# Layer norm statistics of four of sixteen token tiles moved from VectorE to ScalarE, in the routing rounds of a Golay and top-2 expert kernel

## The chip, the cores and the metric

The kernel runs on one core of one Trainium2 chip. The metric is the device time of one execution in microseconds (us). Three executions of the kernel before took 1242.68, 1247.49 and 1249.14 us; their median is 1247.49 us. The engines are TensorE (PE), VectorE (DVE), ScalarE (ACT), GpSimd (POOL) and SyncE (SP, which here only starts transfers).

## The reference

`x` has 16 x 1024 tokens of 512 features. Every token is normed, goes through a frequency filter with a 24-bit code correction, and through its two best of eight experts:

```
xn = (x - mean(x)) / sqrt(var(x) + 1e-5)
x1 = real(ifft(fft(xn) * filt))                     # filt from the first 1024 values of xn
bits = sigmoid(x1 @ W_el + b_el) > 0.5              # 24 bits, Golay-corrected
s = x1 + corrected @ W_le + b_le
probs = softmax(xn @ router_w.T)                    # 8 experts, top 2 kept
g = silu(sum over the 2 of (xn @ expert_e + prob_e) * weight_e)
out = x + s * g
```

## The kernel before, in words

The 16384 tokens are 128 tiles of 128 tokens. There are three stages.

**Set-up**, up to some 30 us: filter tables, weights of the router.

**Routing rounds**, up to some 305 us. There are R = 8 rounds of U = 4 steps, a step being a block of GT = 4 tiles (128 x 2048 values, 1 MB). Every engine runs its own `step1(i, k)` for round i and step k, in program order, and waits on semaphores only.

- SP loads block k of round i into `xbuf[:, k]` (`load`, L378). There are only four block buffers, so a load waits until TensorE has turned the block that lies there (`t1_done`) and until its statistics are taken (`stats_ready`). In rounds 2 to 7 the order is block 0, block 1, one expert's weights, block 2, block 3.
- TensorE, in `step1(i, k)`: turns the first two tiles of the next block (L1266), does the product with the router and latent weights of this block (`logits`, L1306), turns the other two tiles of the next block, and turns the result back (L1315). `logits` waits until ScalarE has copied all four turned tiles of its block. At k = 2 it also ranks the tokens of the round before (`rank`, L1323), for which it waits for `pairs` from VectorE.
- ScalarE copies the turned tiles of the next block from PSUM (`turn_copy`, L586), two before and two after the copy of this block's result (`latT_copy`, L632). Between steps it has the norms of the expert weights (`norm`, L592; one in step 0 of each of rounds 1 to 5), the exponentials (L636) and the root of the variance (L670).
- VectorE takes the statistics of a tile by one `bn_stats` (`stat`, L907). In step 0 it runs `choose(i - 1)` (L971 to L999, bits and top 2 of the round before), a chain of small operations, and puts the twelve `stat` of blocks 1 to 3 of round i between them. In step 1 it works out the variances (`deviations`) and then combines one expert's weights (`halves`). In step 2 `place(i - 1)` gives each token its slot (L1038), with the four `stat` of block 0 of the next round beside it; it waits for `rank`. Step 3 is `weigh(i - 1)`.
- GpSimd writes the token numbers into a table in DRAM by sixteen small scatters a round (L493), as soon as the slots of the round are there.

Behind the last round GpSimd's last scatters, two gathers of that table and some index work lead to the first gather of the next stage.

**Expert tiles**, from some 305 us to the end: 28 extra and 128 main tiles of tokens gathered by expert pair. The change doesn't touch them. They use `inf2` as a buffer, which the routing rounds don't use.

Of the kernel before, what the change touches and what calls it, by code (L numbers as in the profile page):

```python
# [10 lines left out]
BF16 = mybir.dt.bfloat16  # L11
# [13 lines left out]
GT = 4  # L25
U = 4
# [52 lines left out]
def build(nc, x_in, W_el, b_el, W_le, b_le, router_w, experts, consts, out):  # L79
# [37 lines left out]
    with ctx:  # L117
# [3 lines left out]
        def sem(name):  # L121
# [116 lines left out]
        to_tile = latT[:, 1, 0:2 * NT].rearrange("p (h t) -> p h t", h=2)  # L238
        onehot = xT4[:, :, :, :].rearrange("p b c n -> p (b c n)")[:, 0:T * 2 * NE].rearrange(
            "p (t s e) -> p t s e", s=2, e=NE)  # L240
        info_bits = info[:, :, 16:64].bitcast(BF16).rearrange("p t (g c) -> p t g c", g=3)


# [32 lines left out]
        def sems(names):  # L276
            return [sem(x) for x in names.split()]
# [13 lines left out]

        t1_done, t1_copied, mm1_done, latT_copied, back_done, lat_copied = sems(
            "t1_done t1_copied mm1_done latT_copied back_done lat_copied")
        stats_ready, aggr_ready, var_ready, sd_ready, newton, rstd_ready = sems(
            "stats_ready aggr_ready var_ready sd_ready newton rstd_ready")
        route_a, route_c, route_d, dx_ready, exp_ready, corr_ready, bits_copied = sems(
# [30 lines left out]
        def after(eng, s, v):  # L327

            if isinstance(v, int) and v <= 0:
                return  # L330
            eng.wait_ge(s, v)
# [41 lines left out]
        @block.sync  # L373
        def _(sp):
            def load(i, k):
                after(sp, t1_done, GT * ((i - 1) * U + k + 1))
                after(sp, stats_ready, (i - 1) * U + k + 1)
                sp.dma_start(xbuf[:, k], x_tiles[:, i, k * GT:(k + 1) * GT, :]).then_inc(ld_x[k], 16)  # L378

            def load_expert(e):  # L380
                if e == LH:
                    sp.wait_ge(pool_halves, 1)
                after(sp, wpm_ready, e - LH)
                after(sp, norm_ready, e - LH + 1)
                sp.dma_start(raw[:, e % LH], experts[e].rearrange("(c p) o -> p c o", p=P)).then_inc(ld_w[e % LH], 16)

            sp.dma_start(x01, x_rows[0:2, :].rearrange("n e -> (n e)").partition_broadcast(P)).then_inc(ld_x01, 16)
            sp.dma_start(rtr, router_w).then_inc(ld_router, 16)
            load(0, 0)
            sp.dma_start(cst[:, :], consts).then_inc(ld_cst, 16)  # L390
            sp.dma_start(welraw, W_el.rearrange("(c p) n -> p c n", p=P)).then_inc(ld_small, 16)
            sp.dma_start(bel[:, :], b_el.partition_broadcast(P)).then_inc(ld_small, 16)
            load(0, 1)
            sp.wait_ge(zeroed, 1)
            for g in range(3):
                sp.dma_start(wle[32 * g:32 * g + GOLAY_N, :], W_le).then_inc(ld_small, 16)
                sp.dma_start(wle[32 * g + GOLAY_N:32 * g + GOLAY_N + 1, :], b_le.rearrange("(a e) -> a e", a=1)).then_inc(ld_small, 16)
            load_expert(0)
            load_expert(1)
            load(0, 2)  # L400
            load(0, 3)
            sp.wait_ge(ld_cst, 16)
            table = pair_tokens.rearrange("(p h r) c -> p h (r c)", p=P, h=FILLS)
            for h in range(FILLS):
                sp.dma_start(table[:, h], cst[:, 0:TROWS // FILLS].bitcast(I32)).then_inc(far_stored, 16)
            load(1, 0)
            load(1, 1)
            load(1, 2)
            load_expert(2)
            load(1, 3)  # L410
            load_expert(3)
            for i in range(2, R):
                for k in range(U):
                    load(i, k)
                    if k == 1 and i + 2 < NE:
                        load_expert(i + 2)

            def turn_main(i, k):
                m, b = (i - XR) * U + k, k % 2
                sp.wait_ge(split_ready, i * U + k + 1)  # L420
                sp.sem_inc(split_seen, 1)
                sp.wait_ge(bits_in, m + 1)
                sp.sem_inc(bits_seen, 1)
                if first_main(i) and k < 2:
                    sp.wait_ge(x_done, NX - 4 + k + 1)
                else:
                    sp.wait_ge(y_done, m - 1)
                sp.sem_inc(y_seen, 1)
                sp.dma_start_transpose(facing[b], parts[b]).then_inc(turned[b], 16)

            def extra_sum(i, k):
                m = (i - XR) * U + k
                if not first_main(i):
                    sp.wait_ge(t_ready, m - U + 1)
                    sp.sem_inc(sum_seen, 1)
                which = sp.value_load(tile_exp[0:1, 2, bass.ds(m, 1)], min_val=0, max_val=NX - 1)
                sp.dma_start(ebuf[:, k], extra_dram[bass.ds(which, 1)].rearrange("o p e -> p (o e)")).then_inc(ld_e[k], 16)

            def step(i, k, last=False):
                if not (last and k + 2 >= U):  # L440
                    turn_main(*at(i, k, 2))
                    extra_sum(*at(i, k, 2))
            for n in range(NX):
                if NX <= n + 3 < NX + 2:
                    turn_main(*at(n // U, n % U, 3))
                sp.wait_ge(acc_ready, n + 1)
                sp.dma_start(extra_dram[n], acc2[:, n % 2]).then_inc(extra_stored[n % 2], 16)
            sp.wait_ge(tiles_ready, 3)
            for b in range(2):
                sp.wait_ge(extra_stored[b], 16 * (NX // 2))  # L450
            extra_sum(XR, 0)
            extra_sum(XR, 1)
            main_rounds(sp, step)
# [126 lines left out]
        def _(act):  # L580
# [69 lines left out]

            NORM_AT = {(0, 2): 2, (1, 0): 3, (2, 0): 4, (3, 0): 5, (4, 0): 6, (5, 0): 7}

            def step1(i, k, last):
                ahead = not (last and k + 1 >= U)
                if ahead and not turned_early(i, k):
                    turn_copy(*at(i, k, 1), 0)
                    turn_copy(*at(i, k, 1), 1)
                latT_copy(i, k)
                if ahead and not turned_early(i, k):
                    turn_copy(*at(i, k, 1), 2)  # L660
                    turn_copy(*at(i, k, 1), 3)
                if i >= 2 and k == 0:
                    info_store(i - 2)
                if (i, k) in NORM_AT:
                    norm(NORM_AT[i, k])
                if i >= 1 and k == 1:
                    exps(i - 1)
                if k == 2:
                    act.wait_ge(var_ready, i + 1)
                    nc.scalar.activation(rt1[:, 1], rt1[:, 0], ACT.Sqrt).then_inc(sd_ready, 1)  # L670
                    if i >= 1:
                        bits_copy(i - 1)
# [82 lines left out]
        def _(dve):  # L755
# [103 lines left out]
                            ALU.subtract).then_inc(c_lo_ready, 1)  # L859

            V.tensor_copy(nbefore[:, :], nbefore_c)
            V.tensor_copy(used[:, :], region_c).then_inc(sort_init, 1)
            dve.wait_ge(iota_ready, 1)
            link(V.tensor_copy(tokf[:, :], tok[:, 1, :]))
# [46 lines left out]
            def deviations(i):  # L911


                dve.wait_ge(stats_ready, U * (i + 1))
                mean_e, sq_e, mean_o, sq_o = (st6[:, :, c] for c in (1, 2, 4, 5))
                V.tensor_tensor(dev[:, 0], mean_e, mean_o, ALU.subtract)
                V.tensor_tensor(dev[:, 1], sq_e, sq_o, ALU.add)
                V.tensor_tensor(dev[:, 2], mean_e, mean_o, ALU.add).then_inc(aggr_ready, 1)
                dve.wait_ge(aggr_ready, 2 * i + 1)
                V.scalar_tensor_tensor(dev[:, 3], dev[:, 0], 0.25, dev[:, 0], ALU.mult, ALU.mult)  # L920
                V.tensor_scalar(dev[:, 1], dev[:, 1], 1.0 / E, EPS, ALU.mult, ALU.add).then_inc(aggr_ready, 1)
                dve.wait_ge(aggr_ready, 2 * i + 2)
                V.tensor_tensor(rt1[:, 0], dev[:, 1], dev[:, 3], ALU.add).then_inc(var_ready, 1)
# [125 lines left out]
            def step1(i, k, last):  # L1049
                following = NONE if last else tiles_of(i + 1, 0)  # L1050
                if i >= 1 and k == 0:
                    choose(i - 1, beside=tiles_of(i, 1) + tiles_of(i, 2) + tiles_of(i, 3))
                if k == 1:
                    if i == 0:
                        for tile in tiles_of(i, 1) + tiles_of(i, 2) + tiles_of(i, 3):
                            tile()
                    deviations(i)
                    if i + 2 < NE:
                        halves(i + 2 if i else 1)
                if i >= 1 and k == 2:  # L1060
                    place(i - 1, (i - 1) % 2, (i - 1) // 2, beside=following)
                if k == 3:
# [386 lines left out]
```

## Time and profile before

| | |
|---|---|
| median of three runs | 1247.49 us |
| profiled execution, its own time | 1248.74 us |
| its span on the core | 1246.9 us |
| busy in the span: TensorE, VectorE, GpSimd, ScalarE | 90%, 87%, 70%, 41% |
| granted TensorE clock, mean | 0.954 |

The span is the time between the first and the last recorded instruction; 1.8 us of the execution's time lie outside of it. Shares over the whole span say little here, since the change sits in the routing rounds alone, which are the stretch from about 30 to 243 us. So the profile is read by stretches and by the order in time of single rows.

### The profile page before, as it was taken

To read this page: it belongs to the slowest core of one execution; us is meant where nothing else is said; L and a number is where in the kernel's file an instruction comes from. 1 tells how busy PE (TensorE), PEld (TensorE's weight loads), DVE (VectorE), ACT (ScalarE), POOL (GpSimd) and SP (SyncE) were. 2 spreads that over 40 slices of the span, in tenths; PEclk is the share of its full clock that TensorE was granted. 3 is DMA by queue.
4 is the path that set the end of the run, shared out by engine and by line. 5 is a ranking of instruction groups with operands and counts; after the bars stand their busy time and mean duration, and the time that the engine had idled before them with its cause. 6 is when DMAs were issued, how large, how long until landed. Compare 5 with 4: busy or idle time off the path is not lost. (4 is left out here: it accounts for less than half of the span.)

```text
span 1246.9 us, 26774 instructions
## 1 busy us (share of the span) xinstructions
PE 1122.4 (90%) x6265; PEld 608.3 (49%) x6266; DVE 1089.1 (87%) x2625; ACT 509.0 (41%) x1151; POOL 877.0 (70%) x873
## 2 busy tenths in 40 slices
PE   5998889700799999999999999999999999999996
PEld 4554555400355455555555554555555555555553
DVE  6799979992888689989999998999999899999985
ACT  4576556560577333323333333333333333333332
POOL 1126654765888378778888887888888788888874
PEclk8999889955799999999999999999999999999999
DMA  8659999300465576666666666666666666666664
GB/s 320 238 192 200 195 168 214 64 18 24 129 185 184 143 167 174 173 168 177 172 171 176 176 173 170 169 172 177 174 174 172 167 178 172 178 170 173 177 168 108
DMA packets 217433, 208.75 MB, mean 167 GB/s; under 512 B 166783, under 2 KB 166783, under 8 KB 213298
## 3 DMA queue, kind: packets, MB, share of 16 engines
q1 hardware_dynamic: 184370, 124.31, 42.2%
q0 software_dynamic: 31872, 79.79, 21.6%
q10 hardware_dynamic: 1152, 4.19, 1.4%
q8 instruction: 17, 0.28, 0.1%
q14 instruction: 22, 0.18, 0.1%
HBM read 123.36 MB, written 47.12 MB: 137 GB/s over the span
## 5 line engine op out<-in xcount | busy, mean ns | idle before, releaser
L1366 PE MATMUL banks<-w_hi,arena 128*128 (+1 forms) x1136 | 431.6, 380 | 9.5 <-DMA arena<-arena 5.0
L1367 PE MATMUL banks<-w_lo,arena 128*128 (+1 forms) x1136 | 431.3, 380 | 0.0
L1368 PE MATMUL banks<-w_hi,arena 128*128 (+1 forms) x1136 | 431.1, 379 | 0.0
L700 ACT ACTIVATE arena<-xbuf,inf 128x512 f16<-128x512 f32 x156 | 112.6, 722 | 509.6 <-DVE xbuf L1168 509.6
L516 POOL DMA_INDIRECT inf<-token_info,gidx x156 | 194.7, 1248 | 54.1 <-issue 54.1
L514 POOL DMA_INDIRECT xbuf<-in_L_attn_x,gidx x156 | 176.3, 1130 | 77.4 <-issue 67.0
L493 POOL DMA_INDIRECT pair_tokens<-tok,slot x128 | 133.8, 1045 | 122.7 <-DVE slot L1038 81.0
L554 POOL TENSOR_TENSOR xbuf<-xbuf 128x512 f32<-128x512 f32 x128 | 162.7, 1271 | 40.1 <-DVE xbuf L1237 35.9
L1366 PEld LDWEIGHTS banks<-w_hi,arena 128*128 128x128 f16 x1136 | 111.2, 98 | 136.7 <-issue 15.0
L1368 PEld LDWEIGHTS banks<-w_hi,arena 128*128 128x128 f16 x1136 | 111.4, 98 | 131.5 <-issue 0.8
L520 POOL DMA_INDIRECT out<-xbuf,sidx x128 | 140.4, 1097 | 40.7 <-issue 40.4
L1367 PEld LDWEIGHTS banks<-w_lo,arena 128*128 128x128 f16 x1136 | 111.2, 98 | 117.1 <-issue 0.6
L1164 DVE TENSOR_TENSOR xbuf<-xbuf 128x256 f32<-128x256 f32 x156 | 141.6, 908 | 13.7 <-DMA inf<-token_info,gidx 13.7
L1174 DVE SCALAR_TENSOR_TENSOR arena<-xbuf,inf,arena 128x512 f16<-128x512 f32 x156 | 117.0, 750 | 19.2 <-ACT arena L700 13.0
L1306 PE MATMUL banks<-xT,wcat 128*128 128x512 f32 x256 | 120.8, 616 | 0.8 <-issue 0.4
L1217 DVE SCALAR_TENSOR_TENSOR arena<-banks,cab,arena 128x512 f32<-128x512 f32 x128 | 95.6, 747 | 13.1 <-PE banks L1368 12.3
L1237 DVE TENSOR_TENSOR xbuf<-xbuf,arena 128x512 f32<-128x512 f32 x128 | 88.7, 693 | 20.7 <-DVE xbuf L1231 7.7
L1208 DVE SCALAR_TENSOR_TENSOR arena<-banks,cab,arena 128x512 f32<-128x512 f32 x128 | 95.9, 749 | 7.9 <-DMA arena<-extra_sums 4.1
L1231 DVE TENSOR_TENSOR xbuf<-xbuf 128x256 f32<-128x256 f32 x256 | 97.5, 422 | 4.4
L734 ACT ACTIVATE arena<-arena,inf 128x512 f32<-128x512 f32 x128 | 91.1, 712 | 3.8 <-DVE arena L1217 3.8
L907 DVE BATCH_NORM_STATS2 st<-xbuf 128x6 f32<-128x512 f32 x128 | 86.0, 684 | 7.1 <-DMA xbuf<-in_L_attn_x 7.1
L1266 PE MATMUL banks<-ident,xbuf 128*128 128x128 f32 x512 | 74.1, 293 | 17.0 <-DMA xbuf<-in_L_attn_x 16.8
(284 smaller groups left out, 1713.5 us busy)
## 6 DMA issues: line engine op xcount, KB each, us to landing
xbuf<-in_L_attn_x SPq DMA_DIRECT2D x32, 1024.0 KB, 13.7
arena<-extra_sums SPq DMA_DIRECT2D x128, 256.0 KB, 2.7
arena<-in_L_ffn_expert_weights SPq DMA_DIRECT2D x8, 1024.0 KB, 11.7
extra_sums<-arena SPq DMA_DIRECT2D x28, 256.0 KB, 2.1
token_info<-info ACTq DMA_DIRECT2D x8, 512.0 KB, 12.8
xbuf<-in_L_attn_x,gidx POOLq DMA_INDIRECT x156, 3.6
inf<-token_info,gidx POOLq DMA_INDIRECT x156, 2.8
pair_tokens<-tok,slot POOLq DMA_INDIRECT x128
```

The source lines that it names most:

```text
L493: pool.indirect_dma_start(out=pair_slots, out_offset=bass.IndirectOffsetOnAxis(ap=slot[:, buf, t:t + 1], axis=0), in_=tok[:, buf, t:t + 1] ...
L514: pool.indirect_dma_start(out=x2[:, k], out_offset=None, in_=x_rows, in_offset=tokens, bounds_check=N - 1, oob_is_err=False).then_inc(ld_x ...
L516: pool.indirect_dma_start(out=inf2[:, k], out_offset=None, in_=info_dram, in_offset=tokens, bounds_check=N - 1, oob_is_err=False).then_inc ...
L520: pool.indirect_dma_start(out=out_rows, out_offset=bass.IndirectOffsetOnAxis(ap=sidx[:, k:k + 1], axis=0), in_=o2[:, k % 2], in_offset=Non ...
L554: G.tensor_tensor(o2[:, b], sg2[:, b], x2[:, k], ALU.add).then_inc(o_ready, 1)
L700: nc.scalar.activation(hi4[ring(i, k)], uv2[:, b], ACT.Copy, scale=inf2[:, k, 1:2]).then_inc(hi_ready, 1)
L1164: V.tensor_tensor(raw2[:, b, 0:H], x2[:, k, 0:H], x2[:, k, H:E], ALU.add).then_inc(raw_ready, 1)
L1174: V.scalar_tensor_tensor(lo4[ring(i, k)], uv2[:, b], inf2[:, k, 1:2], hi4[ring(i, k)], ALU.mult, ALU.subtract).then_inc(split_ready, 1)
L1306: last = mm(psum[:, 2], wcat[:, c], xT4[:, k % 2, c], start=(c == 0), stop=(c == C - 1))
L1366: mm(ps, hi[:, c], wh, start=(c == 0), stop=False)
L1367: mm(ps, hi[:, c], wl, start=False, stop=False)
L1368: end = mm(ps, lo[:, c], wh, start=False, stop=(c == C - 1))
```

## The change

Of the sixteen tiles of a round, the four of block 3 get their mean and their sum of squared deviations from ScalarE. For each, one pass `Copy` with scale 1/512 adds up to the mean, and a second pass `Square` of (mean - x) adds up to the squared deviations. The values that the passes write go to `inf2`, which nothing reads then. `bn_stats` gives two means and two sums for a tile (even and odd values); ScalarE's passes give one of each, so the mean is written twice and the second sum stays zero.

The passes for tiles 0 and 1 of the block stand in ScalarE's step 0, those for tiles 2 and 3 in its step 1, around the copies that were there. VectorE's step 1 does `halves` first and `deviations` after it, the latter with waits for ScalarE's passes.

```
         def _(sp):
             def load(i, k):
                 after(sp, t1_done, GT * ((i - 1) * U + k + 1))
-                after(sp, stats_ready, (i - 1) * U + k + 1)
+                if k < U - 1:
+                    after(sp, stats_ready, (i - 1) * (U - 1) + k + 1)
+                else:
+                    after(sp, squares_ready, GT * i)
...
+            def tile_mean(i, q):
+
+                if q == 0:
+                    act.wait_ge(ld_x[U - 1], 16 * (i + 1))
+                    after(act, var_ready, i)
+                after(act, squares_ready, GT * i + q)
+                nc.scalar.activation(squares, xbuf[:, U - 1, q], ACT.Copy, scale=1.0 / E,
+                                     accum_out=st6[:, SHARE + q, 1:2]).then_inc(means_ready, 1)
+
+            def tile_square(i, q):
+
+                act.wait_ge(means_ready, GT * i + q + 1)
+                nc.scalar.activation(squares, xbuf[:, U - 1, q], ACT.Square, bias=st6[:, SHARE + q, 1:2], scale=-1.0,
+                                     accum_out=st6[:, SHARE + q, 2:3]).then_inc(squares_ready, 1)
+                if q == GT - 1:
+                    nc.scalar.activation(st6[:, SHARE:, 4], st6[:, SHARE:, 1], ACT.Copy).then_inc(pairs_alike, 1)
+
             def step1(i, k, last):
                 ahead = not (last and k + 1 >= U)
-                if ahead and not turned_early(i, k):
-                    turn_copy(*at(i, k, 1), 0)
-                    turn_copy(*at(i, k, 1), 1)
-                latT_copy(i, k)
-                if ahead and not turned_early(i, k):
-                    turn_copy(*at(i, k, 1), 2)
-                    turn_copy(*at(i, k, 1), 3)
+                turns = ahead and not turned_early(i, k)
+                for h in range(2):
+                    if k < 2:
+                        tile_mean(i, 2 * k + h)
+                    if turns:
+                        turn_copy(*at(i, k, 1), 2 * h)
+                    if k < 2:
+                        tile_square(i, 2 * k + h)
+                    if turns:
+                        turn_copy(*at(i, k, 1), 2 * h + 1)
+                    if h == 0:
+                        latT_copy(i, k)
...
             def deviations(i):
 
 
-                dve.wait_ge(stats_ready, U * (i + 1))
+                dve.wait_ge(stats_ready, (U - 1) * (i + 1))
+                dve.wait_ge(squares_ready, GT * (i + 1))
+                dve.wait_ge(pairs_alike, i + 1)
...
             def step1(i, k, last):
                 following = NONE if last else tiles_of(i + 1, 0)
                 if i >= 1 and k == 0:
-                    choose(i - 1, beside=tiles_of(i, 1) + tiles_of(i, 2) + tiles_of(i, 3))
+                    choose(i - 1, beside=tiles_of(i, 1) + tiles_of(i, 2) + [None] * GT)
                 if k == 1:
                     if i == 0:
-                        for tile in tiles_of(i, 1) + tiles_of(i, 2) + tiles_of(i, 3):
+                        for tile in tiles_of(i, 1) + tiles_of(i, 2):
                             tile()
-                    deviations(i)
                     if i + 2 < NE:
                         halves(i + 2 if i else 1)
+                    deviations(i)
```

On ScalarE, between the end of step 0 and that of step 1 of round 2, the order before is this (`xT` is the turned block, `latT` the result, `w_lo` the norm's waste, the table load that of the exponential):

```order
L649 DMA token_info<-info 128x1024
L592 ACTIVATE w_lo,norm<-arena 128x2048
L586 ACTIVATE xT<-banks 128x4x128 x2
L632 ACTIVATE latT<-banks 128x512
L586 ACTIVATE xT<-banks 128x4x128 x2
L636 ACT_TABLE_LOAD
```

At the same place the changed kernel has the following, where `inf,st<-xbuf` are the new passes and L591 is the former L586:

```order
L654 DMA token_info<-info 128x1024
L597 ACTIVATE w_lo,norm<-arena 128x2048
L666 ACTIVATE inf,st<-xbuf 128x512
L591 ACTIVATE xT<-banks 128x4x128
L672 ACTIVATE inf,st<-xbuf,st 128x512
L591 ACTIVATE xT<-banks 128x4x128
L637 ACTIVATE latT<-banks 128x512
L666 ACTIVATE inf,st<-xbuf 128x512
L591 ACTIVATE xT<-banks 128x4x128
L672 ACTIVATE inf,st<-xbuf,st 128x512
L675 ACTIVATE st<-st 128x4
L591 ACTIVATE xT<-banks 128x4x128
```

A pass on `xbuf` now stands ahead of each of the four copies to `xT`, two of them ahead of `latT` and two behind it.

On VectorE, the end of `choose(0)` and what follows it up to `place(0)` is this before (`st<-xbuf` are the statistics, `dev` and `rt` belong to `deviations`, `arena` and `w_lo` to `halves`):

```order
L998 SCALAR_TENSOR_TENSOR rsm<-rsm 128x16
L907 BN_STATS st<-xbuf 128x6
L999 TENSOR_TENSOR pairs<-rsm,cst 128x448
L916 TENSOR_TENSOR dev<-st 128x16
L917 TENSOR_TENSOR dev<-st 128x16
L918 TENSOR_TENSOR dev<-st 128x16
L920 SCALAR_TENSOR_TENSOR dev<-dev 128x16
L921 TENSOR_SCALAR dev<-dev 128x16
L923 TENSOR_TENSOR rt<-dev 128x16
L1043 TENSOR_TENSOR arena<-arena 128x1024
L1045 TENSOR_TENSOR arena<-arena 128x1024
L1046 TENSOR_TENSOR w_lo<-arena 128x512
```

In the changed kernel the same place reads:

```order
L1030 SCALAR_TENSOR_TENSOR rsm<-rsm 128x16
L1031 TENSOR_TENSOR pairs<-rsm,cst 128x448
L1075 TENSOR_TENSOR arena<-arena 128x1024
L1077 TENSOR_TENSOR arena<-arena 128x1024
L1078 TENSOR_TENSOR w_lo<-arena 128x512
L1079 TENSOR_TENSOR w_lo<-arena 128x512
L948 TENSOR_TENSOR dev<-st 128x16
L949 TENSOR_TENSOR dev<-st 128x16
L950 TENSOR_TENSOR dev<-st 128x16
L952 SCALAR_TENSOR_TENSOR dev<-dev 128x16
L953 TENSOR_SCALAR dev<-dev 128x16
L955 TENSOR_TENSOR rt<-dev 128x16
```

The statistics between the last operations of the chain are gone, and `deviations` has moved behind the four operations of `halves`.

## Rows read from the trace of the kernel before

**Rows 1.** Busy time by stretch; columns PE, PEld, DVE, ACT, POOL, clock, DMA share, GB/s

```profile
57.00:111.00 54.00, 49.85 (x242) 30.10 (x240) 53.38 (x160) 35.89 (x62) 18.26 (x18) 1.00 0.67 184
111.00:196.00 85.00, 73.58 (x331) 45.11 (x329) 77.12 (x224) 52.57 (x89) 45.66 (x47) 0.90 1.00 175
196.00:243.00 47.00, 43.98 (x206) 25.87 (x204) 45.84 (x163) 29.18 (x51) 32.86 (x35) 1.00 0.72 147
```

**Rows 2.** Who waited for whom, 60 to 245 us; total, times, longest

```profile
PE banks L1266 <- DMA xbuf<-in_L_attn_x: 8.1, 3, 4.2
PE banks L1323 <- DVE pairs L999: 6.2, 4, 2.2
ACT latT L632 <- PE banks L1306: 49.4, 21, 4.8
```

**Rows 3.** Timeline of TensorE, round 2: start, duration, what, idle before

```profile
86.53 3.60 PE L1306 MATMUL banks<-xT,wcat 128*128 128x512 f32 x8
...
92.22 3.60 PE L1306 MATMUL banks<-xT,wcat 128*128 128x512 f32 x8
98.06 0.36 PE L1323 MATMUL banks<-pairs,nbefore 128*128 128x448 f16 x1 [2.23 <-DVE pairs L999]
```

**Rows 4.** Timeline of ScalarE, round 2, step 1

```profile
85.11 1.92 ACT L592 ACTIVATE w_lo<-arena 128x2048 bf16<-128x2048 f32 x1
86.92 0.21 ACT L592 ACTIVATION_READ_ACCUMULATOR w_lo<-arena 128x1 f32 x1
87.01 1.09 ACT L586 ACTIVATE xT<-banks 128x512 f32<-128x512 f32 x2
90.16 0.60 ACT L632 ACTIVATE latT<-banks 128x512 f32<-128x512 f32 x1 [2.06 <-PE banks L1306]
90.66 1.08 ACT L586 ACTIVATE xT<-banks 128x512 f32<-128x512 f32 x2
```

**Rows 5.** Page, costliest groups: a ScalarE pass of 512 from SBUF

```profile
L700 ACT ACTIVATE arena<-xbuf,inf 128x512 f16<-128x512 f32 x156 | 112.6, 722 | 509.6 <-DVE xbuf L1168 509.6
```

**Rows 6.** Timeline of VectorE, round 0: sixteen statistics in a row

```profile
29.70 9.58 DVE L907 BATCH_NORM_STATS2 st<-xbuf 128x6 f32<-128x512 f32 x16
```

**Rows 7.** Loads of block 3 of rounds 2, 3, 4, 7: issue, then landing

```profile
L378 SPq DMA_DIRECT2D xbuf<-in_L_attn_x x1: 328/328/328, 72.8 to 72.8; - x1
DMA to landing us min/median/max: 4.9/4.9/4.9
...
L378 SPq DMA_DIRECT2D xbuf<-in_L_attn_x x1: 328/328/328, 99.5 to 99.5; - x1
DMA to landing us min/median/max: 13.7/13.7/13.7
...
L378 SPq DMA_DIRECT2D xbuf<-in_L_attn_x x1: 328/328/328, 127.1 to 127.1; - x1
DMA to landing us min/median/max: 21.2/21.2/21.2
...
L378 SPq DMA_DIRECT2D xbuf<-in_L_attn_x x1: 327/327/327, 213.3 to 213.3; - x1
DMA to landing us min/median/max: 17.1/17.1/17.1
```

**Rows 8.** Timeline of TensorE: products of (3, 1), (4, 1), (7, 1), (7, 2)

```profile
113.20 3.60 PE L1306 MATMUL banks<-xT,wcat 128*128 128x512 f32 x8
...
144.66 5.63 PE L1306 MATMUL banks<-xT,wcat 128*128 128x512 f32 x8
...
226.20 3.60 PE L1306 MATMUL banks<-xT,wcat 128*128 128x512 f32 x8
231.89 3.60 PE L1306 MATMUL banks<-xT,wcat 128*128 128x512 f32 x8
```

**Rows 9.** Timeline of GpSimd: first scatter of round 6, last of round 7

```profile
240.33 0.99 POOL L493 DMA_INDIRECT pair_tokens<-tok,slot  x1 [1.60 <-DVE slot L1038]
...
292.75 0.95 POOL L493 DMA_INDIRECT pair_tokens<-tok,slot  x1 [0.30 <-issue]
```

More of the change, by code:

```diff
@@ L240, in build @@
             "p (t s e) -> p t s e", s=2, e=NE)
+        squares = inf2[:, :, :].rearrange("p k w -> p (k w)").bitcast(BF16)
         info_bits = info[:, :, 16:64].bitcast(BF16).rearrange("p t (g c) -> p t g c", g=3)
@@ L293, in build @@
             "t1_done t1_copied mm1_done latT_copied back_done lat_copied")
+        means_ready, squares_ready, pairs_alike = sems("means_ready squares_ready pairs_alike")
         stats_ready, aggr_ready, var_ready, sd_ready, newton, rstd_ready = sems(
@@ L651, in _ @@
             NORM_AT = {(0, 2): 2, (1, 0): 3, (2, 0): 4, (3, 0): 5, (4, 0): 6, (5, 0): 7}
+            SHARE = (U - 1) * GT
+            def tile_mean(i, q):
[11 more added lines that the diff above has]
+                    nc.scalar.activation(st6[:, SHARE:, 4], st6[:, SHARE:, 1], ACT.Copy).then_inc(pairs_alike, 1)
             def step1(i, k, last):
                 ahead = not (last and k + 1 >= U)
-                if ahead and not turned_early(i, k):
-                    turn_copy(*at(i, k, 1), 0)
-                    turn_copy(*at(i, k, 1), 1)
-                latT_copy(i, k)
-                if ahead and not turned_early(i, k):
-                    turn_copy(*at(i, k, 1), 2)
-                    turn_copy(*at(i, k, 1), 3)
+                turns = ahead and not turned_early(i, k)
[10 more added lines that the diff above has]
+                        latT_copy(i, k)
                 if i >= 2 and k == 0:
@@ L861, in _ @@
             V.tensor_copy(nbefore[:, :], nbefore_c)
+            V.memset(st6[:, (U - 1) * GT:, 5], 0.0)
             V.tensor_copy(used[:, :], region_c).then_inc(sort_init, 1)
```

## The prediction

> **What bounds the kernel now.** I read busy time by stretch first [rows 1]. From 57 to 111 us VectorE is busy for 53.38 of 54 us: it paces rounds 1 and 2. From 111 to 196 us no engine is full (TensorE 73.58 and VectorE 77.12 of 85 us) while the share of the DMA engines is 1.00: the loads of x pace rounds 3 to 5. From 196 to 243 us TensorE has 43.98 and VectorE 45.84 of 47 us, close together. ScalarE is never above 36 of 54 us, and that share misleads. The list of waits shows why [rows 2]: ScalarE's largest wait, 49.4 us in 21 pieces, is for TensorE's product, and TensorE's waits are for blocks of x (8.1 us) and for `pairs` (6.2 us). TensorE and ScalarE run in a tight alternation: product, copy of the result, the last two copies of the next block, next product.
>
> How tight shows in one step of round 2 [rows 3, 4]. The product starts at 86.53 and the next at 92.22, 5.69 us later. ScalarE's last copy ends at 90.66 + 1.08 = 91.74, or 5.21 us after the product's start. Only some 0.4 us are free there if 0.1 is left for the handing over. At step 2, TensorE then waits 2.23 us for `pairs` [rows 3]; this wait is what VectorE costs in rounds 1 and 2.
>
> **What the change takes from VectorE.** Sixteen statistics in a row took 9.58 us, 0.60 each [rows 6]. Four fewer in a round are 2.4 us, and less in practice, since they filled gaps of a dependent chain. Below, it can be worth nothing where VectorE doesn't pace. `halves` ahead of `deviations` costs nothing: the combined order is the same length, and what waits for the variance (the root in ScalarE's step 2) stands behind the copies of that step. VectorE's new wait for ScalarE's squares ends when ScalarE's step 1 does; behind it are `place` and the rank's result, which come after the product of step 2 anyway.
>
> **What it puts on ScalarE.** The trace before has no pass of 512 values with a sum. The nearest rows: a plain copy of 512 (0.60 us, the next starts 0.50 later), the expert norm with its sum, whose reading of the accumulator adds 87.01 - 86.92 = 0.09 [rows 4], and a pass of 512 from SBUF with a pointer operand, 0.722 [rows 5], some 0.62 by the same overlap. So one pass takes 0.59 to 0.71. If nothing overlapped, it would be 0.72 + 0.21 = 0.93. I take 1.3 us for a pair (mean and square) because the overlap shows in every row, and keep 1.2 and 1.9 as its ends. The Trainium skill, page "ScalarE: Activation LUTs", section "What ACT_TABLE_LOAD costs", gives 186 ns + 0.833 per value, 93 more with a pointer operand and 93 less back to back. By it a pair would be an estimated 1.13 us without the reading of the accumulator, and the sum below +9.9 instead of +10.4.
>
> In steps 0 and 1 one pair stands between the copy of the result and the last copy. The last copy then ends 5.21 + 1.3 = 6.5 us behind the product's start, and the next product starts at 6.6 instead of 5.69: +0.9 us. In step 1 of rounds 1 to 5 the norm (1.9 us) and the other pair also lie ahead of the copy of the result. The idle time there is 2.06 us [rows 4], of which 86.53 - 85.11 = 1.4 came from the norm starting ahead of the product. With ScalarE as the last to release the product, that lead is gone down to 0.1 and the pair takes 1.3, so the copy comes some 0.5 late: +1.4 for this step. A round gains 2.3 us in this alternation (1.8 in rounds 6 and 7), which eats the 2.23 us of waiting for `pairs`. **Rounds 1 and 2 thus come out even**, and the gain on VectorE is not seen.
>
> **The new wait, and the term that decides.** ScalarE's first pass of a round waits for block 3 of that round, and it stands ahead of all copies of step 0. Before, block 3 was first needed two steps later by TensorE. Queued behind that wait are the copies of block 1 and of the result, so TensorE can't start the product of step 1. After the landing come two pairs (2.6), four copies (2 x 1.09) and the copy of the result (0.5): 5.3 us. Hence product (i, 1) starts 5.3 us after block 3 lands, at the earliest. The loads [rows 7] against the products [rows 8], if they land as before:
> round 3: 99.5 + 13.7 = 113.2, product at 118.5 instead of 113.20, +5.3;
> round 4: 127.1 + 21.2 = 148.3, product at 153.6 instead of 144.66, +8.9;
> round 7: 213.3 + 17.1 = 230.4, product at 235.7 instead of 226.20, +9.5.
> In round 2 the block lands at 72.8 + 4.9 = 77.7, well ahead of that round's step 0, whose norm starts at 85.11 [rows 4], so it costs nothing. The Trainium skill, page "DMA: Bandwidth & Descriptors", section "Rules for kernel authors", advises to issue a transfer early and to wait on its semaphore late. The change waits two steps earlier than before; the rows of rounds 3, 4 and 7 agree with that rule, and by it alone the sign would be slower too.
>
> From product (7, 1) to (7, 2) there are 6.6 us instead of 5.69, so (7, 2) starts at 242.3 instead of 231.89: **+10.4 us**. Behind (7, 2) come the rank of round 6, its slots and the 32 last scatters. The first of them had waited 1.60 us for the slots, and GpSimd is busy with them until 292.75 [rows 9]; nothing there is early enough to wait less, and the shift goes through to the end one to one.
>
> Do the landings stay? The load of (7, 3) is issued behind the turning of (6, 3), so it goes out later by what round 6 is late; between the shifts of rounds 3 and 4 I take 6 us, so 219.3, but it goes into a shorter queue. With 4.9 and 17.1 us as ends of its time it lands at 224.2 to 236.4. The late end gives product (7, 1) at 241.7 and +16.4 in all. At the early end the alternation decides: from 153.6, three rounds of 4 x 5.69 + 0.7 (two rank products) + 1.8 to 2.3, 25.6 us each, give 230.4 at (7, 1) and +5.1 in all. The middle of the two is 10.8, and the unchanged landing gives 10.4, which I take. A pair at 1.9 us would add 1.2 in the landing term and 0.6 in the step: +12.2.
>
> The sum: 1248.74 (the profiled execution's own time) + 10.4 = 1259.1. That execution lies 1.25 us above the median of the three, so I forecast **1258 us**.
>
> **Rivals.**
> *VectorE's gain comes through*: faster. It decides if block 3 lands ahead of the end of every round, and the pair hides in the 0.4 us free and the 2.23 us wait. Rounds 1 to 3 then give 2.4 us each; rounds 4 to 7, which loads or TensorE pace, little: 1247.5 - 7 = 1240. For it speaks VectorE at 99% early; against it the landings at 113.2 and 148.3. Chance 0.10.
> *Loads hide it*: block 2 is free earlier, since the chain of `choose` is shorter by 2.4 us, and the scatters, which lie beside the slow loads, are shifted against them. Loads that land 5 to 8 us earlier in rounds 4 to 7 take the shift down to 2 to 5: 1250. Against it speaks that the share of the DMA engines was already 1.00, so there is no room to catch up. Chance 0.18.
> *The wait feeds on itself*: a later product (i, 2) frees buffer 3 later, the load goes out later, the next round's pass waits longer. A round then lasts the time of the load plus 5.3 + 7.1 + 4.6 = 17 us (4.6 from the product to the end of the turning behind it). With 13.7 that is 30.7 against 25.6, so two such rounds at the end add 10: 1268. The queue must stay as long as before for it. Chance 0.12.
> The forecast has 0.60.
>
> **How the numbers follow.** Forecast's own range: +5 to +16, so 1253 to 1264. The 8 in 10 range takes in most of the second rival and the low half of the third: 1249 to 1267. A measurement tells 0.5%, 6.2 us, from no change. Slower by more: nearly all of the forecast (0.58) and the third rival (0.12), 0.70. Within: second rival and the rest, 0.20. Faster: 0.10.
>
> **What would show it.** Right: ScalarE's first pass of rounds 3, 4 and 5 waits for the load of x, by some 5 to 10 us each; product (i, 1) starts 5.3 us after the landing; steps 0 and 1 without a wait take 6.6 us and 6.6 to 7.1; TensorE's waits name ScalarE's copies and no longer `pairs`; the first scatter of round 6 is at 251 instead of 240.33; VectorE has idle time in rounds 1 and 2; the tile stage is as long as before. Wrong: a pass that takes more than 0.95 us or a table load beside the passes; landings of block 3 ahead of step 0 in rounds 4 and 5; a wait of VectorE for the squares that delays `place`; another length of the stretch between the first scatter of round 6 and the last of round 7, 52.4 us before.

## The result

| | before | changed |
|---|---|---|
| median of five runs on the same chip | 1248.18 us | 1259.66 us |
| lowest and highest | 1242.68, 1251.39 | 1255.4, 1266.17 |
| profiled execution, its own time | 1248.74 us | 1255.4 us |
| its span | 1246.9 us | 1253.6 us |

The ratio is 1.0101, with a 95% interval from 1.0056 to 1.0146: slower, by 11.5 us in the medians, where 1258 us and a range from 1249 to 1267 had been forecast. The profiled execution is the shortest of its five and only 6.7 us longer than that of before. Its routing rounds still lose 12.6 us up to product (7, 2), where 10.4 had been forecast; part of it is given back behind them, as shown below.

The page of the changed kernel: the span, and the busy time of each engine. ScalarE has 550.0 us of work.

```profile
span 1253.6 us, 26894 instructions
...
PE 1130.1 (90%) x6265; PEld 609.1 (49%) x6266; DVE 1078.2 (86%) x2594; ACT 550.0 (44%) x1287; POOL 875.2 (70%) x873
```

Busy time by stretch, columns as in [rows 1]. The stretches are bounded by products that start a round: rounds 1 and 2, rounds 3 to 5, and what follows. Two short ones lie around the product of step 1 of round 7.

```profile
56.30:108.00 51.70, 47.68 (x230) 28.73 (x229) 50.52 (x151) 45.16 (x94) 17.86 (x18) 1.00 0.71 204
108.00:196.50 88.50, 76.35 (x345) 44.80 (x344) 74.05 (x226) 68.53 (x141) 46.87 (x49) 0.94 0.90 181
196.50:256.00 59.50, 49.81 (x208) 28.47 (x206) 40.83 (x142) 40.23 (x86) 31.80 (x34) 0.91 0.57 101
230.00:235.00 5.00, 1.99 (x14) 1.69 (x13) 5.00 (x16) 4.41 (x11) 3.82 (x4) 0.78 0.02 1
236.00:240.00 4.00, 4.00 (x7) 1.70 (x7) 1.94 (x8) 2.04 (x6) 3.08 (x4) 0.55 0.73 28
241.00:245.00 4.00, 3.19 (x23) 2.29 (x22) 0.81 (x6) 3.57 (x9) 2.37 (x3) 1.00 0.02 0
```

In rounds 1 and 2 VectorE is busy for 50.52 of 51.70 us. That looks like its limit but isn't: with the same work on VectorE and no passes, these rounds take 47.2 us (the relief alone, below). In rounds 3 to 5 no engine is full, and the share of the DMA engines has gone down to 0.90: another thing than the loads holds back the rounds too. The list of waits from 60 to 262 us names it (columns as in [rows 2]):

```profile
ACT latT L637 <- PE banks L1338: 21.7, 13, 3.4
...
ACT inf L666 <- DMA xbuf<-in_L_attn_x: 19.0, 5, 4.9
DVE tokf L1059 <- PE banks L1356: 16.0, 6, 3.6
DVE dev L948 <- ACT st L675: 15.1, 4, 6.0
...
PE banks L1347 <- ACT latT L637: 13.7, 12, 3.0
PE banks L1338 <- ACT xT L591: 11.1, 14, 0.9
```

TensorE's waits for the loads and for `pairs` are gone. It waits for ScalarE's two kinds of copies, 24.8 us in all, and ScalarE waits for the load of x: five times (once in each of rounds 3 to 7), 19.0 us, the longest 4.9. ScalarE's idle time for the product fell from 49.4 us to 21.7.

Timeline of ScalarE: the passes of step 0 of round 2, and then the first pass of rounds 3, 4 and 7, each with the wait ahead of it.

```profile
81.68 0.65 ACT L666 ACTIVATE inf<-xbuf 128x512 bf16<-128x512 f32 x1
82.20 0.22 ACT L666 ACTIVATION_READ_ACCUMULATOR inf<-xbuf 128x1 f32 x1
82.29 0.61 ACT L591 ACTIVATE xT<-banks 128x512 f32<-128x512 f32 x1
82.77 0.74 ACT L672 ACTIVATE inf<-xbuf,st 128x512 bf16<-128x512 f32 x1
83.38 0.22 ACT L672 ACTIVATION_READ_ACCUMULATOR inf<-xbuf,st 128x1 f32 x1
83.48 0.61 ACT L591 ACTIVATE xT<-banks 128x512 f32<-128x512 f32 x1
...
111.40 0.63 ACT L666 ACTIVATE inf<-xbuf 128x512 bf16<-128x512 f32 x1 [3.77 <-DMA xbuf<-in_L_attn_x]
...
142.84 0.63 ACT L666 ACTIVATE inf<-xbuf 128x512 bf16<-128x512 f32 x1 [4.27 <-DMA xbuf<-in_L_attn_x]
...
230.59 0.63 ACT L666 ACTIVATE inf<-xbuf 128x512 bf16<-128x512 f32 x1 [4.91 <-DMA xbuf<-in_L_attn_x]
```

From the start of a pass to the next instruction it is 0.61 us for the mean (81.68 to 82.29) and 0.71 for the square (82.77 to 83.48): 1.32 for a pair. The reading of the accumulator adds 0.09 to 0.10 of each. The Trainium skill, page "ScalarE: Activation LUTs", section "What ACT_TABLE_LOAD costs", gives an estimated 1.13 us for the two passes without that reading; with 0.19 us from the rows for two readings it comes to the measured 1.32.

TensorE's products at the same places (steps 0 to 2 and the rank of round 2, then (3, 1), (4, 1), (7, 1) and (7, 2)):

```profile
82.18 3.60 PE L1338 MATMUL banks<-xT,wcat 128*128 128x512 f32 x8
88.75 3.70 PE L1338 MATMUL banks<-xT,wcat 128*128 128x512 f32 x8 [0.71 <-ACT xT L591]
95.79 3.70 PE L1338 MATMUL banks<-xT,wcat 128*128 128x512 f32 x8 [0.92 <-ACT xT L591]
99.33 0.35 PE L1355 MATMUL banks<-pairs,nbefore 128*128 128x448 f16 x1
...
116.62 5.40 PE L1338 MATMUL banks<-xT,wcat 128*128 128x512 f32 x8 [0.83 <-ACT xT L591]
...
148.06 6.77 PE L1338 MATMUL banks<-xT,wcat 128*128 128x512 f32 x8 [0.83 <-ACT xT L591]
...
235.84 5.53 PE L1338 MATMUL banks<-xT,wcat 128*128 128x512 f32 x8
244.44 3.70 PE L1338 MATMUL banks<-xT,wcat 128*128 128x512 f32 x8 [0.81 <-ACT xT L591]
```

These answer to [rows 3, 8]. The two steps of round 2 take 6.57 and 7.04 us, and the rank waits for nothing. The products of step 1 start 5.22, 5.22 and 5.25 us after the first pass behind the landing.

GpSimd: first scatter of round 6, last of round 7, first gather of the tokens' table, first gather of the tile stage.

```profile
252.90 0.96 POOL L498 DMA_INDIRECT pair_tokens<-tok,slot  x1 [8.92 <-DVE slot L1070]
...
300.62 0.96 POOL L498 DMA_INDIRECT pair_tokens<-tok,slot  x1 [0.30 <-issue]
303.68 0.97 POOL L511 DMA_INDIRECT tokT<-pair_tokens,trow  x1 [2.10 <-issue]
...
312.48 1.01 POOL L519 DMA_INDIRECT xbuf<-in_L_attn_x,gidx  x1 [6.57 <-ACT gidx L723]
```

The last of these rows answers to the following of the kernel before:

```profile
305.52 1.02 POOL L514 DMA_INDIRECT xbuf<-in_L_attn_x,gidx  x1 [6.57 <-ACT gidx L694]
```

The shift of 12.6 us at the first scatter (252.90 against 240.33 in [rows 9]) is 7.9 at the last and 7.0 at the first gather of the tile stage. The tile stage behind it has 941.1 us in this profile and 941.4 in that of before.

### The profile page after: what moved, and what is told of

The parts are those of the page before. It is cut to its first block and busy times, and to the rows that moved or that the text cites. A ratio compares the mean times of both kernels' runs of the same rounds, so it can differ in the third digit from the quotient of the medians.

```text
span 1253.6 us, 26894 instructions
## 1 busy us (share of the span) xinstructions
PE 1130.1 (90%) x6265; PEld 609.1 (49%) x6266; DVE 1078.2 (86%) x2594; ACT 550.0 (44%) x1287; POOL 875.2 (70%) x873
## 5 line engine op out<-in xcount | busy, mean ns | idle before, releaser
L498 POOL DMA_INDIRECT pair_tokens<-tok,slot x128 | 129.0, 1008 | 136.5 <-DVE slot L1070 95.3
L1338 PE MATMUL banks<-xT,wcat 128*128 128x512 f32 x256 | 128.1, 647 | 12.4 <-ACT xT L591 12.0
L1206 DVE SCALAR_TENSOR_TENSOR arena<-xbuf,inf,arena 128x512 f16<-128x512 f32 x156 | 117.1, 751 | 18.4 <-ACT arena L729 12.6
L1249 DVE SCALAR_TENSOR_TENSOR arena<-banks,cab,arena 128x512 f32<-128x512 f32 x128 | 95.6, 747 | 13.1 <-PE banks L1400 11.1
L759 ACT ACTIVATE xbuf<-banks 128x384 f32<-128x384 f32 x128 | 62.5, 488 | 59.1 <-PE banks L1448 58.9
L1338 PEld LDWEIGHTS banks<-xT,wcat 128*128 128x128 f32 x256 | 50.2, 207 | 68.6 <-issue 53.1
```

The costliest lines, as they stand in the source:

```text
L498: pool.indirect_dma_start(out=pair_slots, out_offset=bass.IndirectOffsetOnAxis(ap=slot[:, buf, t:t + 1], axis=0), in_=tok[:, buf, t:t + 1] ...
L1206: V.scalar_tensor_tensor(lo4[ring(i, k)], uv2[:, b], inf2[:, k, 1:2], hi4[ring(i, k)], ALU.mult, ALU.subtract).then_inc(split_ready, 1)
L1338: last = mm(psum[:, 2], wcat[:, c], xT4[:, k % 2, c], start=(c == 0), stop=(c == C - 1))
```

## The experiments

Theory A, that of the prediction: what costs time is ScalarE's wait for block 3 two steps earlier than before, with the copies queued behind it. Rival B: the passes' own time in the alternation of TensorE and ScalarE. Rival C: the relief of VectorE is worth something, and other things hide it. Each ratio is to the kernel before, run in turn with the others of its group; the expectations in us were made against 1247 to 1248 us, so the ratios are what to compare. A difference of ratios is given in percentage points. The first two groups ran on one chip, the third on another.

### First group (the kernel before: 1241.86 us, median of 29 runs)

**The wait alone.** The kernel before, with one wait more ahead of ScalarE's step 0.

```diff
             def step1(i, k, last):
+                if k == 0:
+                    act.wait_ge(ld_x[U - 1], 16 * (i + 1))
```

> The kernel before, and in ScalarE's step 0 of every round one wait more, for the landing of block 3, ahead of the first copy; no pass is added and VectorE keeps all sixteen statistics. Theory (the early wait is what costs): product (i, 1) starts 2.8 us behind the landing of block 3 (four copies 2.2, the result's 0.5, hand-over 0.1), which with the landings of before is +2.9 us in round 3, +6.4 in round 4 and +7 in round 7: 1254 us, 1252 to 1257. Rival (the passes between the copies are what costs): nothing, 1248 us.

Measured 1249.48 us, ratio 1.0056 (1.0029 to 1.0083). Its waits, and its ScalarE at round 3 with the product that follows:

```profile
ACT xT L586 <- DMA xbuf<-in_L_attn_x: 23.0, 5, 7.1
```

```profile
110.19 0.60 ACT L586 ACTIVATE xT<-banks 128x512 f32<-128x512 f32 x1 [5.30 <-DMA xbuf<-in_L_attn_x]
```

```profile
113.11 5.30 PE L1308 MATMUL banks<-xT,wcat 128*128 128x512 f32 x8
```

The wait costs 0.56% without any new work. It lasts longer in all than in the changed kernel (23.0 against 19.0 us), but the product of step 1 follows 2.9 us after it instead of 5.2, since no passes stand between. These rows are from one of its shorter executions, 1242.69 us.

**Passes without the wait.** The changed kernel, its passes reading a constant that lies in SBUF. It leaves out the true statistics of block 3.

```diff
                 if q == 0:
-                    act.wait_ge(ld_x[U - 1], 16 * (i + 1))
+                    act.wait_ge(ld_cst, 16)
-                nc.scalar.activation(squares, xbuf[:, U - 1, q], ACT.Copy, ...
+                nc.scalar.activation(squares, cst[:, 0:E], ACT.Copy, ...
```

> The changed kernel, whose eight passes of a round read 512 columns of the constants instead of the tiles of block 3, so that they wait for no load of x; the statistics of block 3 are those of the constants, so they and what hangs on them aren't the reference's. Number, length and place of the passes stay. Theory (the early wait costs most): the longer alternation alone, +0.9 us in a step 0, up to +1.4 in a step 1, which rounds 1 to 5 have in hand and rounds 6 and 7 pay with 1.8 each: 1248 to 1253 us, most likely 1251. Rival (the passes cost): 1259 us, as the changed kernel.

Measured 1238.66 us, ratio 0.9970 (0.9940 to 0.9999). With the same passes, copies and order, the slowdown is gone, and ScalarE waits for no load of x. The expectation (the time of before or up to 0.4% more) had left out what VectorE gains. From the list of waits:

```profile
ACT latT L637 <- PE banks L1338: 24.9, 16, 3.4
...
PE banks L1338 <- ACT xT L591: 10.6, 14, 0.9
```

TensorE waits for the copies of `xT` as long as in the changed kernel (10.6 against 11.1 us). This is what the passes do in the alternation, and it is not where the slowdown comes from.

**The relief alone.** The kernel before without VectorE's four statistics of block 3, which are constants instead; there are no passes. The load of block 3 no longer waits for statistics either, so this too is in what is measured.

```diff
-                    choose(i - 1, beside=tiles_of(i, 1) + tiles_of(i, 2) + tiles_of(i, 3))
+                    choose(i - 1, beside=tiles_of(i, 1) + tiles_of(i, 2) + [None] * GT)
```

> The kernel before without the four statistics of block 3 on VectorE and without anything in their place: their table entries are constants (mean 0, variance 1), so these tokens are normed by them. It is the most that any way of moving these four tiles off VectorE could give. Theory (VectorE paces rounds 1 to 3 only, then loads and TensorE do): 2 us in each of these rounds, part of it given back to the loads: 1241 to 1247 us, most likely 1245. Rival (VectorE is the bound of all rounds): 7 x 2.4 = 17 us less, 1231 us. Second rival (loads pace from round 3 and take all of it back): 1248 us.

Measured 1233.24 us, ratio 0.9943 (0.9913 to 0.9974). VectorE's share is worth 0.57% when nothing is put in its place. The kernel above, with the passes, has 0.27 points less of it, though the two intervals overlap. Where the passes take it back shows in rounds 1 and 2, from product (1, 0) to (3, 0): the kernel before, the relief alone, and the passes without the wait (columns as in [rows 1]):

```profile
55.80:106.80 51.00, 46.85 (x231) 28.42 (x230) 50.48 (x139) 35.30 (x61) 16.32 (x16) 1.00 0.64 195
```

```profile
53.90:101.10 47.20, 46.59 (x230) 28.46 (x229) 46.41 (x130) 35.25 (x61) 17.20 (x16) 1.00 0.67 215
```

```profile
55.70:107.40 51.70, 47.70 (x231) 28.74 (x230) 50.53 (x151) 45.50 (x96) 17.89 (x18) 1.00 0.71 206
```

The relief alone takes 3.8 us off these two rounds, and with the passes they last 51.7 us, as in the changed kernel.

**All passes of a step ahead of the result's copy.** The changed kernel in another order.

```diff
-                        turn_copy(*at(i, k, 1), 2 * h)
+                        turn_copy(*at(i, k, 1), h)
                     if k < 2:
                         tile_square(i, 2 * k + h)
-                    if turns:
-                        turn_copy(*at(i, k, 1), 2 * h + 1)
-                    if h == 0:
-                        latT_copy(i, k)
+                latT_copy(i, k)
+                if turns:
+                    turn_copy(*at(i, k, 1), 2)
+                    turn_copy(*at(i, k, 1), 3)
```

> The changed kernel with all four passes of a step ahead of the copy of the result, so that only that copy and two others stand between a product and the next. Theory (the wait for the landing costs, the order behind it hardly): the 5.3 us behind a landing stay, since all passes and copies still stand between; a step without a wait takes 5.9 us instead of 6.6: 1 to 3 us less than the changed kernel, 1257 us. Rival (the pair between the result and the last copy is what costs): 15 steps x 0.65 = 10 us less than the changed kernel, 1249 us.

Measured 1255.33 us, ratio 1.0103 (1.0053 to 1.0153). The wait stays, and TensorE's waits move from the copies of `xT` (0.4 us left) to the result's copy:

```profile
PE banks L1347 <- ACT latT L637: 21.8, 14, 6.1
...
ACT inf L666 <- DMA xbuf<-in_L_attn_x: 17.2, 4, 6.5
```

The time is that of the changed kernel as far as six executions tell; the 1 to 3 us less that were expected are too small for them. Behind the landing stands the same amount of work in either order.

### Second group, same chip (before: 1239.46 us, median of 26 runs)

**Before and changed kernel again**, unedited, each beside the others of this group.

> The kernel before, unchanged, for a profile beside those of the other three of this group. No difference from the kernel before; first scatter of round 6 and first gather of the next stage as in the first profile within some us, since loads land a little differently in each execution.

> The changed kernel, unchanged, timed beside e7 and e8. 0.9 to 1.2% over the kernel before.

The kernel before took 1244.8 us in its one profiled execution. The changed one had a median of 1250.24 us and gave 1.0101 (1.0063 to 1.0139), the first result once more. Its profiled execution has 13.2 us of waiting for the load, not 19.0, and product (7, 2) at 229.3 us against 228.6 before: a single execution can hide nearly all of the shift, since the landings came early in it (217.3 us in round 7). The same holds for the wait alone, whose profile has the first gather of the tile stage at 295.3 us; the two of the kernel before have it at 305.5 and 298.7, those of the changed kernel at 312.5 and 298.2. So the ratios rest on the medians, and the profiles only show where the waits lie.

**Passes on block 1**, which lands well ahead of block 3. VectorE keeps blocks 0, 2 and 3.

```diff
-                if k < U - 1:
-                    after(sp, stats_ready, (i - 1) * (U - 1) + k + 1)
+                if k != 1:
+                    after(sp, stats_ready, (i - 1) * (U - 1) + max(k, 1))
                 else:
                     after(sp, squares_ready, GT * i)
...
-                    act.wait_ge(ld_x[U - 1], 16 * (i + 1))
+                    act.wait_ge(ld_x[1], 16 * (i + 1))
```

> The changed kernel with ScalarE's passes on block 1 in place of block 3: the same number of passes at the same places, a complete computation, and VectorE keeps blocks 0, 2 and 3 (2 and 3 at their old places in the chain). Block 1 landed ahead of step 0 in each round of the trace before. Theory (the early wait for block 3 is the cost, the relief is worth some 0.5%, the passes cost half of that back): 0.2 to 0.5% under the kernel before, as e2_no_landing. Rival (the buffer of block 1 now comes free only at the end of step 1, up to 9 us later, and the loads queued behind it on SP, an expert's and block 2's, go out late): 0.3 to 1% over the kernel before.

Measured 1246.71 us, ratio 1.0066 (1.0034 to 1.0098). ScalarE's wait for the load is gone from its list, but SP's queue now waits for ScalarE before it may load block 1 again. Its waits:

```profile
SPq L333 <- ACT inf L672: 102.4, 7, 21.1
```

The loads of blocks 2 and 3 stand behind that one. Product (2, 0) starts at 88.3 us here and at 82.2 in the changed kernel; from round 3 on a round takes 25.8 us, in the kernel before of this group 26.6. The stall moved from the taking of a block to its release, and in this profile it hurts in the first rounds alone, where loads had been far ahead.

**No relief.** The changed kernel; VectorE takes the statistics of block 3 as well, into a tile that nothing reads.

```diff
-                ins = V.bn_stats(st6[:, k * GT + q], xbuf[:, k, q])
+                ins = V.bn_stats(spare[:, q] if k == U - 1 else st6[:, k * GT + q], xbuf[:, k, q])
```

> The changed kernel, and VectorE takes the four statistics of block 3 as well, into a spare tile that nothing reads, at their old places in the chain: all that the change adds, without what it takes away. Theory (with the wait for block 3, ScalarE paces the rounds, VectorE's relief is lost): within 0.3% of e6_after_again. Rival (the relief still counts in full): 0.6% over e6_after_again.

Measured 1252.49 us, ratio 1.0101 (1.0070 to 1.0132), the ratio of the changed kernel. With the passes and the wait in the program, freeing VectorE brings nothing that these runs can tell; with these two intervals, less than 0.5% can't be told.

### Third group, another chip (before: 1310.08 us, median of 23 runs)

On this chip the same kernel is 5.5 to 5.7% longer. From round 3 on a round of it takes 37.5 us instead of 25 to 31, and its tile stage 952 us instead of 941 to 949. Numbers of waits there can't be laid beside the others.

**Block 3 for rounds 0 to 2, block 1 from round 3 on**, to have each where it doesn't stall.

```diff
+        def shared(i):
+            return U - 1 if i < 3 else 1
...
-                    act.wait_ge(ld_x[U - 1], 16 * (i + 1))
+                    act.wait_ge(ld_x[b], 16 * (i + 1))
```

> A complete computation: ScalarE's passes work on block 3 in rounds 0 to 2, where it lands in time, and on block 1 in rounds 3 to 7, where block 3 doesn't; VectorE has the other three blocks of each round. It should keep the relief and avoid both costs seen so far, the wait for block 3 and the late freeing of block 1's buffer, which cost e7_block_one 7 us in rounds 0 to 2 and nothing behind (its rounds 2 to 6 took 25.8 us each, against 26.8 in e5_before_again). Theory (these two waits were the whole cost): 5 us or 0.4% under the kernel before. Rival (the passes themselves, between product and copies, take the relief back): within 0.2% of the kernel before.

Measured 1315.11 us, ratio 1.0027 (1.0000 to 1.0054). Inconclusive as a repair: it isn't faster than the kernel before here, and it wasn't tried on the chip of the first two groups.

**The wait one step earlier still.** The kernel before, ScalarE waiting at step 3 for block 3 of the next round.

```diff
+                if k == U - 1 and not last:
+                    act.wait_ge(ld_x[U - 1], 16 * (i + 2))
```

> The kernel before with one wait more on ScalarE, as in e1_wait_only, but one step earlier: block 3 of the next round is waited for in step 3, ahead of its copies. It measures whether such a wait feeds on itself, since the load goes out only behind the product of step 2. Theory (a round then lasts the load's time plus a fixed chain): from the product of step 2 to the load 4.6 us, a load of 7 to 10, to the next product 2.8, three steps of 5.7 and the rank 0.7, in all 32 to 35 us against 26.8, so 5 to 8 us in each of 7 rounds: 35 to 55 us, 2.8 to 4.5% over the kernel before. Rival (the loads catch up, a wait costs once and is made good later): up to 1% over it.

Measured 1312.33 us, ratio 1.0015 (0.9993 to 1.0037): far under the 2.8 to 4.5% of the theory, which was the prediction's third rival (the wait feeds on itself). But it is no test of it here. The theory had rounds of 32 to 35 us against 26.8, and on this chip the kernel before already takes 37.5 us for a round, this one 37.8.

**Before and changed kernel on this chip**, one execution each.

> The kernel before, unchanged, for one more profile: how much the landings of block 3, the scatters behind the last round and the last stage vary from one execution to another. Product (7, 2) within 4 us of 231.9 and 228.6, the two seen.

> The changed kernel, unchanged, for one more profile. In the two seen, product (7, 2) started at 244.4 and 229.3; theory (the landing of block 3 decides, and it varies): between these, and the later, the longer ScalarE waited for block 3 in the rounds before.

1309.21 and 1313.71 us, or +0.3%, by single executions. Product (7, 2) starts at 285.7 and 295.2 us; both expectations had been made from the rounds of the other chip and miss. Busy time by stretch, first of the kernel before, then of the changed one, each two rounds long:

```profile
111.40:186.60 75.20, 53.15 (x231) 32.08 (x230) 53.00 (x160) 35.92 (x61) 32.78 (x33) 0.86 0.68 155
```

```profile
114.00:191.00 77.00, 57.55 (x231) 33.50 (x230) 48.19 (x148) 46.39 (x96) 30.65 (x31) 0.82 0.53 152
```

TensorE and VectorE are each busy for only 53 of 75 us before, and data come at 155 GB/s (in the second group 202, in the kernel before, from 108.7 to 187.3 us). The likely reason is the loads, but it isn't shown: the landings' records are incomplete there, and nothing on this chip varied the loads alone.

The +0.3% doesn't mean that the routing rounds lost nothing there. Product (7, 0) starts at 269.6 us in the changed kernel and at 261.5 in the kernel before, the first scatter of round 6 at 304.4 and 295.3, and the first gather of the tile stage at 362.0 and 355.3. The shift there is 6.7 us, near the 7.0 of the first pair. The tile stage, which the change doesn't touch, was 2.2 us shorter in this execution, 949.9 against 952.1.

## Why the prediction was right

**Taken from VectorE, worth nothing in this kernel: right.** The relief alone is worth 0.57%, about 7 us, as much as the first rival gave to rounds 1 to 3. But with the passes and the wait in the program it is gone: with and without the relief the ratio is 1.0101. Rounds 1 and 2 came out even, as forecast: 51.7 us from product (1, 0) to (3, 0) against 51.0 before, and 47.2 with the relief alone. So the passes eat the gain there, which is what the prediction said. VectorE got less idle time there than "has idle time" suggests, 1.2 of 51.7 us; its busy time there is that of before, 50.5 us, though eight statistics are gone, and no run here says what fills it. Elsewhere it idles for TensorE's rank (16.0 us) and for ScalarE's squares (15.1). The latter did not delay the last `place` here: from product (7, 2) to the first scatter it is 8.46 us, before 8.44.

**Price of the passes: right.** A pair 1.32 us (1.3), step 0 6.57 (6.6), step 1 with its norm 7.04 (7.1). With the relief and without the wait, the passes cost 0.27 points.

**Landing plus 5.3 us: right.** 5.22, 5.22 and 5.25 us in rounds 3, 4 and 7. The kernel with the wait alone shows both parts: 2.9 us behind the landing without passes, 5.2 with them. The parts alone don't add up: wait +0.56%, passes +0.27, relief -0.57, in all +0.26%, and +1.01% measured. Most of the missing 0.75 points is the relief, which brings nothing here that the runs can tell, as the changed kernel without it shows. Wait and passes alone give +0.83%, and the 0.18 points that are left lie within the intervals. The 2.3 us of passes behind each of five landings would be an estimated 11.5 us (0.9%) if each landing paced; the 0.45 points between the wait alone (1.0056) and the kernel without relief (1.0101) are half of that. The Trainium skill, page "DMA: Bandwidth & Descriptors", section "Rules for kernel authors", advises to wait late for a transfer; the kernel with the wait alone agrees on the chip of the first group (+0.56%); on that of the third the wait at step 3 showed no cost that can be told.

**Landings unchanged: half right, and luck in the last.** They came at 111.4, 142.8 and 230.6 us instead of 113.2, 148.3 and 230.4. Block 3 of round 4 was 5.5 us early and that of round 5 9.4 us (172.0 against 181.4), so some catching up took place as in the second rival. Hence product (4, 1) came 3.4 us late and not 8.9. The prediction had argued that a share of 1.00 of the DMA engines leaves no room to catch up; but at that share 175 GB/s were moved [rows 1], and the same kernel moved 202 GB/s at 0.93 in the second group. The load of (7, 3) went out 5.3 us later than before, at 218.6 (219.3 had been taken), and took 12.0 us instead of 17.1. The two nearly cancel, so the landing stood where it was, and the 9.6 us at product (7, 1) met the forecast 9.5. They came late, by the chain of the third rival: from product (6, 1) to (7, 1) it is 30.7 us, before 25.0, made up of 8.5 to product (6, 2), 5.0 to the load behind the turning of (6, 3), 12.0 for the load and 5.2 behind the landing. In the four rounds from (3, 1) to (7, 1) this chain didn't hold throughout: product (5, 1) was only 1.9 us later than before. The waits were 2.2 to 4.9 us, not "5 to 10 each".

**From (7, 1) to (7, 2) 6.6 us: mis-sized, 8.60.** The products behind a stall took 5.40, 6.77 and 5.53 us, before 3.60, 5.63 and 3.60. In the window from 236 to 240 us the granted clock is 0.55, the level of 1.2 GHz for all but its end, and from 241 to 245 it is 1.00, that of 2.4 GHz; ahead of it, from 230 to 235, TensorE was busy for 1.99 of 5 us. The prediction had a row of such a product (5.63 us in [rows 8]) and didn't use it. So (7, 2) started at 244.4 instead of the forecast 242.3, and the first scatter at 252.9 instead of 251.

**"One to one to the end": wrong for the profiled execution.** The 32 scatters took 47.7 us from the start of the first to that of the last, before 52.4, and 5.6 us of the shift were gone at the first gather. Over ten executions outside the third group, the stretch from the first scatter to the first gather had 59.1 to 65.2 us, and the one of before on which the sum was made was the longest. The medians show +11.5, close to the +10.4 of the sum, but in the pair of profiles two errors of opposite sign stand beside each other, the slow product and the scatters, and the last landing was right by luck. The mechanism was right; how near the number came is in part luck.

No kernel here that computes the whole reference beat the one before.

## What to carry to other kernels

An engine's idle share says at most how much work fits in, and not when: give a pass to the idler engine only behind the point where its data are needed anyway, since everything queued behind the wait inherits it. Price a wait together with the work between it and the next engine, and ask whether a gain elsewhere outlives it: here wait, passes and relief alone give +0.26% by their sum and +1.01% in one kernel, mostly since the relief no longer counts. Ask for each buffer both who waits for it to come and who waits for it to be free; moving the passes to another block only changed the one for the other.

## What the runs showed of the hardware

- The same kernel took 1239.5 and 1241.9 us in two groups of runs on one chip and 1310.1 us on another, where a routing round lasted 37.5 us from round 3 on; no run says why.
- The tile stage, identical in all kernels, had 940.7 to 948.7 us in the executions outside the third group, and 949.9 to 953.8 in it. The spread of the former is 8 us, more than half of the effect here, so one profile can't size it; stages have to be compared one by one.
- The tiny scatters of GpSimd went out in 47.7 us in one execution and 52.4 in another, 32 of them in both, behind the same chain. Most took 0.96 us; before, seven of them took 1.9 to 2.6 us, in the changed kernel three 2.0 to 2.6; no run here says why.
